# One-hots of picked rows from codes stored shifted seven times, compared in place; a store and a load on ScalarE's queue; ScalarE's copies one group later

## The reference

```
x = layernorm(x + relu(sum over edges of a * msg, plus self loop))   # L0: a = tanh(relu(score/sqrt(32))), 86 relations, 16 bases
x = layernorm(x + segment_sum(x[src], dst))                          # L1
x = layernorm(x + attention(x, src, dst))                            # L2: softmax over the edges of a node
x = layernorm(x + 10 propagation steps with degree norms)            # L3
```

## Time and profile before

| | |
|---|---|
| median of three runs | 1116.56 us |
| the profiled execution | 1117.4 us, span 1114.8 us, mean granted clock 0.889 |
| busy in the span | PE 911.3, DVE 949.8, ACT 504.3, POOL 589.9 us |
| POOL's gathers | 534, from 11.15 to 761.65 us |
| first `products_of` of the sweep (line 1387) | 71.2 us |
| last one | 767.1 us |

### The profile page before, as it was taken

One profiled execution on the slowest core, in us unless ns is written; L12 is line 12 of the kernel. 1 busy time (PEld: TensorE's weight loads), 2 busy tenths in 40 slices (PEclk: granted clock), 3 DMA queues, 4 the chain that ended last, 5 costly groups with the idle time before them and its releaser, 6 DMA issues.

```text
span 1114.8 us, 56977 instructions
## 1 busy us (share of the span) xinstructions
PE 911.3 (82%) x24130; PEld 866.3 (78%) x24130; DVE 949.8 (85%) x2405; ACT 504.3 (45%) x1244; POOL 589.9 (53%) x546
## 2 busy tenths in 40 slices
PE   3348888988989988887888888876649958999996
PEld 2347878878878877887787787875639958999996
DVE  8869999999999999999999999995469985555556
ACT  0235554655555565666666666665765300000000
POOL 5777777777777777777777777772000000000000
PEclk9559988998998998989999888895778979999998
DMA  4343332332222233223223322320000000000001
GB/s 120 56 77 58 67 58 58 59 68 57 57 60 67 54 62 65 52 57 68 53 58 58 67 57 52 69 39 7 5 2 4 4 3 4 4 4 4 4 5 19
DMA packets 54400, 48.54 MB, mean 44 GB/s; under 512 B 35470, under 2 KB 44142, under 8 KB 54142
## 3 DMA queue, kind: packets, MB, share of 16 engines
q0 software_dynamic: 17088, 8.78, 9.4%
q1 hardware_dynamic: 31390, 15.23, 6.3%
q10 hardware_dynamic: 5664, 20.84, 5.0%
HBM read 42.49 MB, written 2.32 MB: 40 GB/s over the span
## 4 chain that ended last, share of the span: by engine, by line
DVE 41%; PE 35%; ACT 6%; issue 6%; POOL 5%; DMA 4%; SPq 1%; ACTq 1%; DVEq 0%
PE ps L883 14%; DVE arena L1411 9%; DVE arena L1372 8%; POOL arena L631 5%; PE ps L816 4%; PE ps L930 3%; PE ps L765 3%; DVE aggT L1424 3%; DVE arena L1432 3%; PE ps L914 2%; DMA agg_table<-arena 2%; DVE arena L1362 2%; DVE arena L1387 2%; PE ps L804 2%; DVE arena L1391 2%
## 5 line engine op out<-in xcount | busy, mean ns | idle before, releaser
L631 POOL DMA_INDIRECT arena<-x_pad,arena x534 | 588.1, 1101 | 163.0 <-issue 161.5
L816 PE MATMUL ps<-aggT 128*128 128x128 f16 x3472 | 243.3, 237 | 2.0 <-DVE aggT L1424 1.6
L816 PEld LDWEIGHTS ps<-aggT 128*128 128x128 f16 x3472 | 232.0, 109 | 4.3 <-DVE aggT L1424 4.2
L1372 DVE TENSOR_SCALAR arena<-pair_no,arena 128x275 bf16<-128x275 f16 (+2 forms) x784 | 180.8, 286 | 0.0
L883 PE MATMUL ps<-arena,adj_words 128*128 128x64 f16 x5625 | 171.9, 192 | 3.3 <-DVEq L1697 3.2
L883 PEld LDWEIGHTS ps<-arena,adj_words 128*128 128x128 fp8e4 x5625 | 170.5, 97 | 4.6 <-DVEq L1697 3.6
L1411 DVE TENSOR_TENSOR arena<-ps,arena 128x1536 f32<-128x1536 f32 x98 | 171.3, 1748 | 0.2
L1073 ACT ACTIVATE adj_words<-arena 128x500 uint8 x196 | 126.6, 646 | 56.6 <-ACT arena L1048 54.3
L778 PE MATMUL ps<-arena 128*32 128x44 f32 (+4 forms) x7048 | 132.1, 212 | 15.9 <-DVE arena L1411 15.8
L1043 ACT ACTIVATE arena<-ps 128x500 fp8e4<-128x500 f32 x196 | 113.0, 577 | 68.1 <-PE ps L765 66.3
L778 PEld LDWEIGHTS ps<-arena 128*32 128x32 f32 x7048 | 108.2, 112 | 37.4 <-DVE arena L1411 19.9
(11 more groups left out here) (221 smaller groups left out, 1203.3 us busy)
## 6 DMA issues: line engine op xcount, KB each, us to landing
arena<-line_table ACTq DMA_DIRECT2D x48, 344.0 KB
arena<-x_pad,arena POOLq DMA_INDIRECT x534
arena<-pick_table SPq DMA_DIRECT2D x31, 256.0 KB
arena<-line_table ACTq DMA_DIRECT2D x48, 80.0 KB
arena<-dst_parts SPq DMA_DIRECT2D x196, 5.7 KB
agg_table<-arena SPq DMA_DIRECT2D x196, 2.5 KB
dst_parts<-aggT SPq DMA_DIRECT2D x1, 735.0 KB, 11.3
x<-x_pad SPq DMA_DIRECT2D x1, 400.0 KB
```

The source lines that it names most:

```text
L631: pool.indirect_dma_start(to, None, table, bass.IndirectOffsetOnAxis(ap=index, axis=0)).then_inc(done, 16)
L816: mm = nc.tensor.matmul(ps[:, at:at + PICK_WIDE * FEAT], pick_hot[:, u % PICK_RING, k * P:(k + 1) * P], x_parts[:, t, j * PICK_WIDE:(j + 1 ...
L1372: last = v.tensor_scalar(pair_hot[:, d % 2, k, 0:n], pair_no[:, 0:n], pair_of[:, d * DUO + k // SLOTS, k % SLOTS:k % SLOTS + 1], None, ALU ...
```

## The change

**Codes.** `pick_table` in DRAM holds 7 copies of each pick's 1024 codes, each shifted by another multiple of 128. ScalarE makes them (7 activations over 31 partitions and 1024 columns, into the adjacency matrix's memory, which isn't in use yet), and SP stores them in one DMA when the sweep's branch begins; before, SP stored the one copy as soon as VectorE had made it. VectorE's clearing of a part of that memory (line 1342 before), ScalarE's next line loads and SP's code loads wait for that store.

**One-hots.** A batch of 3, 2 or 2 units is loaded, broadcast to 128 partitions, to the place where its one-hot is to stand (three places, the first in `arena`, the others in `aggT`), and one `tensor_scalar` of 3072 or 2048 columns compares it in place with the partition's number. It stands behind `weigh` in all three duos of a pick; before, the first comparison of a duo stood ahead of `make_last`. Loads of batch n wait until TensorE has used batch n - 3, those of batches 1 and 2 until the parts are stored.

**Queues.** x is loaded on ScalarE's queue and not on SP's, and TensorE's first transposes wait for it alone. The store of the other 20 blocks of parts goes to ScalarE's queue.

**ScalarE's order.** In duo d it copies the counts of groups 2d+1 and 2d+2 (before 2d+2 and 2d+3) and moves pages 2d-1 and 2d (before 2d and 2d+1).

**Small.** `dst_off` is copied once to bf16 (`own_off`, a VectorE copy of 128x784), `last_off_1` is bf16, one more constant is made on POOL.

```diff
@@ -93,8 +92,10 @@
 PICK_READ_AT = {d - 1: c for c, d in enumerate(PICKED)}
-CODES_AT = {c if c < 2 else DUO * PICK_STARTS[c - 1] + SIDES: c for c in range(PICKS)}
-assert len(CODES_AT) == PICKS
+PICK_BATCHES = [units for _, units in sorted(UNITS_AT.items())]
+PICK_PLACES = len(PICK_UNITS[0])
+CODES_AT = {n if n < PICK_PLACES else DUO * (d - PICK_PLACES) + SIDES: n for n, d in enumerate(sorted(UNITS_AT))}
+assert len(CODES_AT) == len(PICK_BATCHES) and max(CODES_AT) < GROUPS and len(set(PICK_UNITS)) == 1
 PICK_TURN = sum(len(units) for units in PICK_UNITS)
@@ -212,7 +213,7 @@
         line_table = nc.dram_tensor("line_table", [2, GROUPED], BF16, kind="Internal").ap()
-        pick_table = nc.dram_tensor("pick_table", [PICKS, DUO * WINDOW], F16, kind="Internal").ap()
+        pick_table = nc.dram_tensor("pick_table", [PICKS, PICK_DEEP, DUO * WINDOW], F16, kind="Internal").ap()
         rel_table = nc.dram_tensor("rel_table", [RELS, REL_ROW], F32, kind="Internal").ap()
...
@@ -268,23 +269,25 @@
 
-        ARENA = 23880
+        ARENA = 23872
         arena = sb("arena", [P, ARENA])
...
         base_t = stay.cut(GROUPS + 1, I32)
-        pair_of, dst_off, last_off_1 = [stay.cut(GROUPS * SLOTS).rearrange("p (g k) -> p g k", k=SLOTS) for _ in range(3)]
+        pair_of = stay.cut(GROUPS * SLOTS).rearrange("p (g k) -> p g k", k=SLOTS)
+        own_off, last_off_1 = [stay.cut(GROUPS * SLOTS, BF16).rearrange("p (g k) -> p g k", k=SLOTS) for _ in range(2)]
         row_twice = stay.cut(2 * GROUPS * SLOTS, BF16).rearrange("p (g k i) -> p g k i", k=SLOTS, i=2)
...
-        codes = stay.cut(2 * DUO * WINDOW, F16).rearrange("p (h e) -> p h e", h=2)
+        first_hot = stay.cut(PICK_UNITS[0][0] * DUO * WINDOW, F16)
         pick_mask = stay.cut(PICKS * WIDE * PICK_WIDE, F16).rearrange("p (c k w) -> p c k w", c=PICKS, k=WIDE)
...
         pick.at = 0
-        pick_hot = pick.cut(PICK_RING * DUO * WINDOW, F16).rearrange("p (j e) -> p j e", j=PICK_RING)
+        pick_hot = [first_hot] + [pick.cut(n * DUO * WINDOW, F16) for n in PICK_UNITS[0][1:]]
+        assert pick.at <= NODES_PAD - 2 * PICK_DEEP * PICK_WIDE * FEAT // 2
         q_parts = aggT[:, 0:BLOCKS * 3 * REL_COLS // 2 + 1].bitcast(BF16)[:, 0:BLOCKS * 3 * REL_COLS]\
...
@@ -306,6 +310,7 @@
         pick_codes = line_parts[0:PICKS, 0, :].bitcast(F16)
+        shifted = Carver(adj_words, ADJ_WORDS).cut(PICK_DEEP * DUO * WINDOW, F16, n=PICKS).rearrange("p (j e) -> p j e", j=PICK_DEEP)
         pick_of = row_of
...
@@ -505,7 +511,7 @@
                 sp.dma_start(to, of).then_inc(edges_loaded, 16)
-            loads = [(x[:], x_pad.rearrange("(b p) f -> p b f", p=P)), (a12[:, 0:FEAT], a1_t), (a12[:, FEAT:2 * FEAT], a2_t),
+            loads = [(a12[:, 0:FEAT], a1_t), (a12[:, FEAT:2 * FEAT], a2_t),
                      (a1_n[:], a1_rows), (a2_n[:], a2_rows), (rel_emb_t[:], rel_emb_cols),
@@ -522,18 +528,17 @@
             sp.dma_start(pick_line, pick_rows).then_inc(pick_loaded, 16)
-            sp.wait_ge(codes_made, 1)
-            sp.dma_start(pick_table, pick_codes).then_inc(codes_stored, 16)
             sp.wait_ge(lines_stored, 16)
...
             sp.dma_start(by_block[:, 0:FIRST_STORED], q_parts[:, 0:FIRST_STORED]).then_inc(first_parts_stored, 16)
-            sp.dma_start(by_block[:, FIRST_STORED:BLOCKS], q_parts[:, FIRST_STORED:BLOCKS]).then_inc(parts_stored, 16)
 
...
                 sp.wait_ge(first_parts_stored, 16)
+                sp.wait_ge(codes_shifted, 1)
+                sp.dma_start(pick_table, shifted).then_inc(codes_stored, 16)
                 sp.wait_ge(codes_stored, 16)
@@ -546,11 +551,14 @@
                     if g in CODES_AT:
-                        c = CODES_AT[g]
-                        if c >= 2:
-                            sp.wait_ge(pick_hots, (c - 1) * PICK_DEEP)
-                        sp.dma_start(codes[:, c % 2, :], pick_table[c:c + 1, :].to_broadcast([P, DUO * WINDOW]))\
-                          .then_inc(code_in[c % 2], 16)
+                        n = CODES_AT[g]
+                        (c, j), deep, place = PICK_BATCHES[n][0], len(PICK_BATCHES[n]), n % PICK_PLACES
+                        if n == 1:
+                            sp.wait_ge(parts_stored, 16)
+                        if n >= PICK_PLACES:
+                            sp.wait_ge(pick_used, j + deep + PICK_DEEP * (c - 1))
+                        sp.dma_start(pick_hot[place], pick_table[c:c + 1, j:j + deep, :].rearrange("c j e -> c (j e)")
+                                     .to_broadcast([P, deep * DUO * WINDOW])).then_inc(code_in[place], 16)
                     if g >= SIDES:
@@ -621,7 +629,8 @@
             numbers(side_no[:, 0:1], [[1, 1]], 0, 1)
-            numbers(pick_no[:], [[P, PICK_DEEP]], 0, 1)
+            numbers(pick_no[:], [[1, 1]], 0, 1)
+            numbers(pick_from[:], [[-P, PICK_DEEP]], 0, 0)
             pool.memset(ident[:], 0.0).then_inc(constants_made, 1)
@@ -702,13 +711,14 @@
         def _(pe):
-            pe.wait_ge(inputs_loaded, 16 * LOADS)
+            pe.wait_ge(x_loaded, 16)
             pe.wait_ge(constants_made, CONSTANTS)
...
+            pe.wait_ge(inputs_loaded, 16 * LOADS)
             nc.tensor.matmul(ps[0:SCORED, SMALL:SMALL + SCORED], a2_n[:], a1_n[:], start=True, stop=True)
@@ -805,15 +815,16 @@
 
-                def pick_unit(c, j):
-                    u = c * PICK_DEEP + j
-                    pe.wait_ge(pick_hots, u + 1)
+                def pick_unit(n, c, j):
+                    at_unit = (j - PICK_BATCHES[n][0][1]) * DUO * WINDOW
+                    pe.wait_ge(pick_hots, n + 1)
                     if j == 0:
...
                         for t in range(2):
-                            mm = nc.tensor.matmul(ps[:, at:at + PICK_WIDE * FEAT], pick_hot[:, u % PICK_RING, k * P:(k + 1) * P],
+                            mm = nc.tensor.matmul(ps[:, at:at + PICK_WIDE * FEAT],
+                                                  pick_hot[n % PICK_PLACES][:, at_unit + k * P:at_unit + (k + 1) * P],
                                                   x_parts[:, t, j * PICK_WIDE:(j + 1) * PICK_WIDE, :]
...
@@ -1013,7 +1024,9 @@
 
+            act.dma_start(x[:], x_pad.rearrange("(b p) f -> p b f", p=P)).then_inc(x_loaded, 16)
             act.wait_ge(inputs_loaded, 16 * LOADS)
+            act.wait_ge(x_loaded, 16)
             act.wait_ge(small_out, 1)
@@ -1031,9 +1044,17 @@
             last.then_inc(rows_made, 1)
+            act.wait_ge(codes_made, 1)
+            for j in range(PICK_DEEP):
+                last = a.activation(shifted[:, j, :], pick_codes, ACT.Identity, bias=pick_from[0:PICKS, j:j + 1])
+            last.then_inc(codes_shifted, 1)
+            act.wait_ge(parts_split, 1)
+            act.dma_start(dst_parts.rearrange("(b p) (j c) -> p b j c", p=P, j=3)[:, FIRST_STORED:BLOCKS],
+                          q_parts[:, FIRST_STORED:BLOCKS]).then_inc(parts_stored, 16)
 
...
                 act.wait_ge(sweep_cleared, 1)
+                act.wait_ge(codes_stored, 16)
                 act.wait_ge(lines_stored, 16)
@@ -1086,8 +1107,7 @@
                 load_lines(act, 2)
-                for g in range(DUO):
-                    copy_counts(g)
+                copy_counts(0)
                 for d in range(DUOS):
@@ -1097,15 +1117,17 @@
                         load_lines(act, c + 2)
-                    if d % BATCH_DUOS == 0 and d >= BATCH_DUOS:
-                        copy_moved(d // BATCH_DUOS - 1)
-                    for g in range(d * DUO, (d + 1) * DUO):
-                        if g + DELAY < GROUPS:
-                            copy_counts(g + DELAY)
-                        move_page(g)
+                    for g in range(d * DUO + 1, (d + 1) * DUO + 1):
+                        if g < GROUPS:
+                            copy_counts(g)
+                        if g >= DELAY:
+                            move_page(g - DELAY)
+                        if g % DUO and d % BATCH_DUOS == 0 and d >= BATCH_DUOS:
+                            copy_moved(d // BATCH_DUOS - 1)
                     for e, at in enumerate(PIECES_FROM):
...
                             count_piece(e * BLOCKS + d - at)
+                move_page(GROUPS - 1)
                 copy_sums(DUOS - 1)
...
@@ -1339,6 +1362,7 @@
                 link(v.memset(square_sums, 0.0))
+                dve.wait_ge(codes_stored, 16)
                 link(v.memset(adj_bytes[:, :, NODES - PAGE:ADJ_COLS], 0))
@@ -1351,7 +1375,7 @@
                     link(v.tensor_tensor(dst_hot[:, c % 2], hot_no[:].unsqueeze(1).to_broadcast(n),
-                                         dst_off[:, c * LINE:(c + 1) * LINE, :].rearrange("p g k -> p (g k)").unsqueeze(2)
+                                         own_off[:, c * LINE:(c + 1) * LINE, :].rearrange("p g k -> p (g k)").unsqueeze(2)
                                          .to_broadcast(n), ALU.is_equal))
@@ -1412,16 +1436,9 @@
 
-                def make_pick_hot(c, j):
-                    u = c * PICK_DEEP + j
```

(40 more changed lines are left out.)

5 lines of the change are left out of this document (2 added, 3 removed).

## The result

The changed kernel takes 1202.42 us (median of 4 runs, 1199.5 to 1204.33), the kernel before 1116.21 in the same comparison: a ratio of 1.0763, 95% interval 1.0724 to 1.0803. Forecast were 1125 us, 1108 to 1134: the direction was right, the size and the cause were not. The profiled execution has a span of 1197.7 us against 1114.8, which is 82.9 more.

A forecast was written before the change was run, and what follows sets the result against it. POOL's gathers were taken as the bound: profiled 1117.4, +12.9 at duo 97 (dearer gathers), -4.7 behind it, gives 1125.6; with that execution 0.8 above the median, 1125 us, range 1108 to 1134.

The forecast's parts named there:

- Hidden at no cost: Work in the sweep and ahead of it, code loads included, said to be covered and to add no time.
- each pick would wait some us: Code loads in the sweep: the cost named if their cover of two duos or 14 us went.
- POOL's chain as the bound: Sweep: POOL's gathers run without a pause and limit duo 97, so VectorE's savings beyond 3.1 us wait for them.
- The gathers' price: POOL's gathers beside longer pick comparisons take longer: 0.5 us a pick, +16 us.
- The prediction's tally: Gather excess per VectorE comparison, from the trace before: 0.39 us at line 1349, 0.10 at line 1424.
- Line 1349's price of 0.39: Mean excess in us of the gather beside each of 47 comparisons of 2048 columns, applied to the new pick comparisons.
- the 62 uncaught ones: Comparisons behind `make_dst_hot` or the last `add_pairs` that cost gathers nothing; support for the rival of no dearer gathers, chance 0.23.
- The start: Ahead of the sweep: the 31-row code store lands at about 74, so VectorE's clearing and sweep start 18.5 us later.
- The tanh: VectorE's waits at line 1404: 10 of the 14 us ahead of duo 97 go, bounds 0 to 14.
- The comparisons: VectorE's pick comparisons in the sweep, 2.24 us a pick instead of 2.80: 17.4 us saved over 31 picks.
- The tail: Behind duo 97: the 5.15 us wait for the tanh goes but for about half a microsecond, -4.7 us.
- it doesn't do what it says: code loads late: Rival in the sweep: code loads late, or a comparison of 3072 out of its fast mode (175 us more); chance 0.02.

The follow-up runs named there:

- e1: Changed kernel with all code loads but the first three issued on ScalarE's queue, two duos ahead; 1206.45 us, ratio 1.0787.
- e6: Changed kernel with 32 rows in the code store and agg stores to separate pages, each waiting only for the store four before; 1112.72 us.
- e8: Kernel before with the agg stores released to separate pages, so none waits for the one before; 1119.78 us, ratio 1.0022.
- e9: Kernel before, stores still waiting for one another, plus 1.5 MB of unused transfers a pick; 1284.46 us, ratio 1.1473.
- e2: Changed kernel with each code load but the first three cut to one unit of 256 KB; 1160.88 us, ratio 1.0370.
- e4: Kernel before with only ScalarE's copies a group later; 1106.12 us, ratio 0.9902.
- e10: e6 with each pick's comparisons cut into seven of 1024 columns, in place; 1119.59 us, ratio 1.0012.
- e11: e4 with the comparison of 2048 columns that makes a line split into two of 1024; 1103.50 us, ratio 0.9878.

## Why the prediction was wrong

*The step that failed* is "Hidden at no cost: ... the code loads (1.8 MB a pick, issued two duos or 14 us ahead ...)". It took the place in the program for the time of issue. The loads stand on SyncE's queue behind stores that each wait for a landing, and it took their bytes to be free beside these. The cost is 71.2 us of waits at the comparisons, and 62.5 us of sweep. Of the two halves of the step the late issue is not what decides: in e1 the codes come in time, and the side rows are late instead. The prediction saw the price of a lost cover ("each pick would wait some us"; it was 2.3) but gave it 2 in 100 without a look at SyncE's waits, which the trace of before has. The line of the stores' wait there, first of before, then of after:

```profile
SPq L543 <- DMA agg_table<-arena: 154.4, 89, 3.7
```

```profile
SPq L548 <- DMA agg_table<-arena: 195.7, 93, 5.7
```

154 us in 89 places: a queue that is already held for a fifth of the sweep. e6 shows that with this wait gone (and the register load) the doubled bytes cost nothing, e8 that the wait without the bytes costs nothing, and e9 that bytes beside the wait are enough, without the merged comparisons. So the chain theory held and volume by itself did not; but the chain costs only with the bytes beside it. How the bytes slow it stays open in part: after, the stores that waited were 0.5 us farther from the one before; in e2 they were not (4.5 us).

*POOL's chain as the bound*: right for the kernel before, as e4 shows (2.4 us from the last gather's end to duo 97), and for e6 (3.4 us, and 13.8 us of waits for gathers). It is not the bound of the changed kernel.

*The gathers' price, +0.5 us a pick, +16 us*: too high by far. The prediction's tally, made on e6's trace, gives 0.14 us for a pick's comparison of 2048 columns, 0.58 for one of 3072 and 0.38 for a line's of 2048: 0.87 a pick, which is 0.18 more than before. Line 1349's price of 0.39 did not go with the size; the same size behind `weigh` had a third of it, as the 62 uncaught ones suggested. In e10 against e6, where only the cut differs, not even the 0.18 is seen in the gathers' mean, and the merged form is the faster. The tally of one trace doesn't carry over well: e11's expectation took 10 us from it, and 28 came, 13 of them where it looked.

*The start, +18.5*: +23.5. The rate of such a transfer was nearly right (444 KB in 21.9 us are 20 GB/s, estimated were 22 to 25); the store was issued at 56.48, 1.9 us later than the first code load before and not 0.6, and most of the rest is the longer landing.

*The tanh, -10*: in the kernel before -15.8 (e4). *The comparisons, -17.4*: with the codes in time (e6 against e10) 5 to 7 us reach the end. *The tail, -4.7*: -3.1.

*The rival "it doesn't do what it says: code loads late"* was the right one, named without a price.

## What to carry to other kernels

A load's lead is the distance from its issue to its use, and issue is decided by all that waits ahead of it on its queue: sum that queue's waits in the trace before calling a load hidden. A chain of small transfers, each waiting for the last one's landing, is paid in latency, and bytes that other transfers put beside it can use up what covered it; here, moving those to another queue did not help. The chain may be covered at first, as it was in the kernel before, and still be the thing that breaks. When a change trades arithmetic for bytes, add the bytes first by themselves.

## What the runs showed of the hardware that was not expected

- A 2.5 KB store allowed the next, which waits for its landing, after 2.6 us at best (2.57 before, 2.65 after). Where the next did wait, it came in the mean 4.4 us behind at 59 GB/s (before, 100 to 700 us), 4.9 at 119 (after) and 5.3 at 103 (e9): not the rate alone decides.
- A transfer of 31 rows of 14 KB took 21.9 us from issue to the next entry of its queue, one of 32 rows 6.9.
- Two comparisons of 1024 columns instead of one of 2048, 48 times, took 28 us off 534 gathers that run beside them on POOL (1089 to 1036 ns). Cutting the picks' comparisons of 3072 and 2048 columns to 1024 took nothing off (1111 to 1115 ns).
